# Decoder layer in float32: the maxima pass one unit behind the other stages, its row one unit earlier, value products one unit later

## What is computed

```python
def _L0_attn_ref(x, Wq, Wk, Wv, Wo):          # 16 heads, head width 32
    q, k, v = proj(Wq), proj(Wk), proj(Wv)
    scores = (einsum(q_r, k_r) + einsum(q_i, k_i)) / sqrt(16)
    scores = where(causal, scores, -inf)
    probs = softmax(scores, axis=-1)
    out = concatenate([probs @ v_r, probs @ v_i], axis=-1)
    return out.transpose(0, 2, 1, 3).reshape(B, N, 2 * C) @ Wo
...
x = x + _L0_attn_ref(_layernorm(x), Wq, Wk, Wv, Wo)
x = x + _L0_xattn_ref(_layernorm(x), ctx_1024, ctx_1024)   # a 16x16 causal softmax over heads, per token
x = x + _L0_ffn_ref(_layernorm(x), kernel, bias, a, b)     # quantized weight plus a low-rank term
```

## Time and profile before

| | |
|---|---|
| median of 3 runs | 923.08 us (922.64 to 927.23) |
| profiled execution | 918.79 us, span 917.0 us |
| TensorE (PE) busy | 708.1 us |
| VectorE (DVE) busy | 659.5 us |
| ScalarE (ACT) busy | 394.0 us |
| GpSimd (POOL) busy | 522.1 us |
| mean granted TensorE clock | 0.91 |

### The profile page before, as it was taken

How to read it: one execution, slowest core, us unless ns; L and a number is a source line. 1 busy time by engine, 2 the same in 40 slices (tenths; PEclk the granted TensorE clock), 3 DMA queues, 4 the chain that set the end, 5 groups by cost and what they waited for, 6 DMA issues and landing times.

```text
span 917.0 us, 14890 instructions
## 1 busy us (share of the span) xinstructions
PE 708.1 (77%) x5099; PEld 469.6 (51%) x5099; DVE 659.5 (72%) x1200; ACT 394.0 (43%) x750; POOL 522.1 (57%) x434
## 2 busy tenths in 40 slices
PE   2679898988898988998898889888989897351023
PEld 2455555745565555565666556655665564140022
DVE  3544354436667876889678977897769777989983
ACT  3114455344534545545544554455444553510101
POOL 4000000033667685668766786678676876867972
PEclk9779999999999989999999999999999998775555
DMA  4786566556575557555655665566565600101000
GB/s 150 101 106 93 70 91 84 104 65 78 78 117 76 75 76 122 75 72 104 100 88 76 103 94 93 78 103 99 66 80 105 99 2 25 40 6 34 0 22 24
DMA packets 47927, 70.46 MB, mean 77 GB/s; under 512 B 4849, under 2 KB 22530, under 8 KB 47874
## 3 DMA queue, kind: packets, MB, share of 16 engines
q1 hardware_dynamic: 46850, 69.52, 49.7%
q10 hardware_dynamic: 1024, 0.26, 0.3%
HBM read 14.98 MB, written 4.19 MB: 21 GB/s over the span
## 4 chain that ended last, share of the span: by engine, by line
PE 45%; DVE 18%; DMA 18%; issue 9%; ACT 7%; POOL 2%; ACTq 0%; DVEq 0%; SPq 0%; POOLq 0%
PE misc L427 22%; DMA stack_q<-max_row 16%; PE acc_bank L427 7%; PE exp_bank L427 6%; PE max_bank L427 6%; DVE head_out L839 4%; DVE neg_max L834 2%; ACT probs L668 2%; PE sum_bank L427 2%; DVE head_scores L839 2%; DVE prod L314 2%; DVE k_lo L896 2%; POOL prod L1093 2%; ACT misc L708 2%; DMA stack_k<-k_lo 1%
## 5 line engine op out<-in xcount | busy, mean ns | idle before, releaser
L668 ACT ACTIVATE probs<-exp_bank 128x512 f32<-128x512 f32 x320 | 188.0, 592 | 242.3 <-PE exp_bank L427 238.8
L1093 POOL TENSOR_TENSOR prod<-head_probs,ctx_sb 128x256 f32<-128x256 f32 (+3 forms) x128 | 236.0, 1876 | 23.9 <-DVE head_out L839 21.9
L834 DVE TENSOR_REDUCE neg_max<-max_bank 128x1 f32<-128x512 f32 (+1 forms) x192 | 130.7, 685 | 95.1 <-PE max_bank L427 94.4
L427 PE MATMUL exp_bank<-stack_q,stack_k 97*128 97x384 f32 (+3 forms) x512 | 151.1, 358 | 38.8 <-DMA stack_q<-max_row 35.5
L314 POOL TENSOR_TENSOR prod<-x1n,ctx_sb 128x256 f32<-128x256 f32 (+2 forms) x112 | 174.9, 1594 | 6.3 <-ACT x1n L638 5.4
L427 PE MATMUL acc_bank<-probs,values 128*32 128x512 f32 (+3 forms) x1024 | 159.3, 452 | 18.2 <-ACT probs L668 14.5
L427 PE MATMUL max_bank<-stack_k,stack_q 96*128 96x384 f32 (+3 forms) x512 | 156.8, 368 | 5.1 <-DVE neg_max L834 4.1
L427 PE MATMUL sum_bank<-probs,ones 128*32 128x512 f32 (+3 forms) x1024 | 159.6, 454 | 0.0
L834 DVE TENSOR_REDUCE seg_max<-max_bank 128x4 f32<-128x512 f32 x128 | 87.1, 687 | 86.4 <-PE max_bank L427 85.2
L1026 POOL TENSOR_TENSOR ln_var<-ln_mv,eps 128x4 f32<-128x4 f32 x24 | 5.2, 218 | 220.6 <-DVE ln_mv L820 220.6
L427 PEld LDWEIGHTS exp_bank<-stack_q,stack_k 97*128 97x128 f32 x512 | 84.6, 195 | 65.1 <-DMA stack_q<-max_row 33.9
(11 more groups left out here) (115 smaller groups left out, 1240.0 us busy)
## 6 DMA issues: line engine op xcount, KB each, us to landing
stack_q<-q_hi SPq DMA_DIRECT2D x64, 256.0 KB, 5.4
stack_k<-k_hi SPq DMA_DIRECT2D x64, 256.0 KB, 8.1
stack_q<-q_lo SPq DMA_DIRECT2D x32, 256.0 KB, 6.6
stack_k<-k_lo SPq DMA_DIRECT2D x32, 256.0 KB, 9.6
x_in<-in_x SPq DMA_DIRECT2D x8, 512.0 KB, 3.5
ctx_sb<-in_ctx SPq DMA_DIRECT2D x32, 128.0 KB, 2.8
x<-in_x SPq DMA_DIRECT2D x8, 512.0 KB, 7.4
out<-y_sb SPq DMA_DIRECT2D x8, 512.0 KB, 3.2
```

What stands on the lines that cost most here:

```text
L427: return nc.tensor.matmul(*args, **kw)
L668: nc.scalar.activation(probs[:, (UNITS * g + n) % PTR, :], exp_bank[n % 2][:, :], ACT.Exp, scale=SCALE).then_inc(exp_done, 1)
L834: vec.tensor_reduce(o, v, axis=AX_X, op=ALU.max, negate=True).then_inc(max_taken, 1)
L1093: last = gp.tensor_tensor(pv_prod[:, COFF[j]:COFF[j + 1]].rearrange("p (q d k) -> p q d k", q=4, k=keys), head_probs[:, 4 * j:4 * j + 4, N ...
```

## The change

The maxima pass runs one unit behind the loop (SHIFT 1), so that only its last unit falls into the next group. The transpose and ScalarE's copy and DMA of the row stand at unit 3, the latter two ahead of the inverses. `attend` runs one unit later (units n - 3 and n - 2 at n = 3, 5, 7, 9; units 8 and 9 at n = 1 of the next group), and so do the copies of `acc_bank` and the sums.

```diff
-    SHIFT = 3
+    SHIFT = 1
...
-                        if st["N"] and n == 0:
+                        if st["N"] and n == 1:
 
                             attend((8, 9), st["N"][1], first_tile - UNITS)
                         if st["C"]:
-                            if n == 2:
+                            if n == 3:
...
-                            if n in (2, 4, 6, 8):
-                                attend((n - 2, n - 1), st["C"][1], first_tile)
+                            if n in (3, 5, 7, 9):
+                                attend((n - 3, n - 2), st["C"][1], first_tile)
...
-                        if st["M"] and n == 4:
+                        if st["M"] and n == 3:
                             pe.wait_ge(max_ready, n_max_ready.up())
                             bank = take(0, max_row_ready, r_row)
...
-                        if st["N"] and n == 1:
+                        if st["N"] and n == 2:
 
                             act.wait_ge(pv_done, n_saved.up(UNITS))
...
+                        if st["M"] and n == 3:
+                            m_slot = st["M"][1]
+                            act.wait_ge(max_psum, n_row.up())
+                            wait(act, max_stacked, n_row_free.up(16) - 32)
+                            copy(max_row[:, m_slot % 2, :], misc[0][0:G * NT, 0:P]).then_inc(max_row_ready, 1)
...
                         if st["N"] and n == 4:
                             act.wait_ge(acc_saved, n_norm.now())
...
-                        if st["M"] and n == 5:
-                            m_slot = st["M"][1]
```

More of the change, by code:

```diff
@@ L693, in body @@
                             layernorm(2, x2, x2n, n - 2)
+                        if st["M"] and n == 3:
[3 more added lines that the diff above has]
+                            copy(max_row[:, m_slot % 2, :], misc[0][0:G * NT, 0:P]).then_inc(max_row_ready, 1)
+                            wait_apart(act, const_ready, (max_row_ready, n_row.now()))
+                            nc.scalar.dma_start(stack_q[STACK:STACK + 1, m_slot, :, :].bitcast(F32),
+                                                max_row[:, m_slot % 2, :].bitcast(F32)).then_inc(max_stacked, 16)
                         if st["N"] and n == 4:
```

## The result

The changed kernel takes 893.44 us (median of 4 runs, 892.81 to 894.8) against 922.86 (median of 4 of the kernel before): a ratio of 0.9684, 95% interval 0.9635 to 0.9732. The forecast was 890.4, range 862 to 912. The profiled execution took 894.05 us with a span of 892.2; the one before had 917.0, so the two traces differ by 24.8 us. The execution profiled before was a quick one: 31 later executions of that kernel took 921.2 to 928.1 us, with a mean granted TensorE clock of 0.906 to 0.896 where the profiled one has 0.910, so against its trace every gain looks some 5 us smaller than by the medians.

A forecast was written before the change was run, and what follows sets the result against it. It took TensorE, waiting for rows that land with their group's six loads, to bound the kernel before a VectorE and GpSimd tail. Seven terms sum to -32.7 us, 918.8 to 886.1; carried over to the median, 890.4 us, range 862 to 912.

The forecast's parts named there:

- Start-up: Before the first scores, the next group's first maxima unit moves ahead of both projections and waits for loads: +4.5 us.
- Wait for the row's copy: TensorE's 15 waits (20.4 us) for ScalarE's copy, which holds the value projection's PSUM bank, go: -18.0 us.
- The cover: Two pairs of units and an attend on TensorE, 2.4 us, hide ScalarE's copy and issue ahead of exponential 4.
- Half clock: TensorE's two 1.2 GHz stretches behind waits for the row's copy go, 1.5 us each: -3.0 us, bounds 0 and -3.4.
- Loads behind k_lo's: In three waiting groups the row overtakes a ctx load issued behind k_lo's, 1.4 us each: -4.2 us.
- nothing ahead of it changes: k_lo's load keeps its issue time, 2.09 us behind the k projection, so the row is issued 0.2 us behind it.
- rival A: The row gets ahead of k_lo's load in most groups, gaining up to 2.0 us each: 857 us, chance 0.20.
- groups with a late VectorE: Only groups where VectorE delays k_lo's load have the row issued ahead of it: 885 us, no separate chance given.
- Waits for `probs`: attend follows its exponential two units behind, not one, saving seven waits of 0.5 us in first groups: -3.7 us.
- costed at nothing: Moved attend calls (same count and banks, older probs), ScalarE's earlier copy and issue, and unit 1's load wait: 0 us.
- Fourth groups: Copy L887 meets shorter GpSimd operations (1.3 us) and the row is earlier (0.4), in four groups: -6.8 us.
- Near the end: TensorE's single 4.6 us wait for the maxima goes, but VectorE bounds right after: -1.5 us, bounds 0 and -4.6.

The follow-up runs named there:

- L887 alone: Kernel before the change, with the four-element copy at source line L887 made by a reduction over one element: 930.12 us, ratio 1.0062.
- the kernel with three edits: Changed kernel with attend calls back at their old units, start-up projections ahead of maxima units, and first groups' x copy and add later: 840.1 us.

## Why the prediction was right, and where it was not

The reading behind the forecast held: a waiting group waits for its six loads, and the row lands with whatever was issued just ahead of it. That the total came out within 3 us is in good part luck, since its parts missed by up to 25 us and cancelled. Point by point:

1. *Start-up*: +5.7 forecast at the first scores and +4.5 behind the next group; +3.6 measured at the first scores, +3.1 left at the fifth group. The cause (projections behind a maxima unit that waits 5.6 us) is shown. The row was forecast between the two k_hi loads; in four other traces it lands there, and the first scores start at 69.2 to 70.0, as forecast (69.3); in the changed kernel's it got ahead of both by luck.
2. *Wait for the row's copy*, -18.0: the wait went, the gain did not. The bank is free, and the step that failed is to book that as time: "nothing else holds that bank" looks at the bank alone. The cover named for ScalarE's copy and issue (2.4 us of TensorE's work) was not enough in first groups, where the copy of x and VectorE's add share the unit. In first groups, 14.9 us of waits went and the groups became 0.8 us longer.
3. *Half clock*, -3.0: between 72 and 700 us the stretches granted 0.50 went from 30.7 to 20.5 us, at most 5 us gained. Right in kind. What was not seen is that it can go the other way, as the runs with SHIFT 1 alone and with L887 alone showed.
4. *Loads behind k_lo's*: the row did pass the ctx loads, but the margin of 0.2 us holds only where VectorE is on time: "nothing ahead of it changes", said of k_lo's load, failed in second groups by 0.74 us. In steady second and fourth groups the row got ahead of k_lo's load, by 0.2 to 0.5 us, and landed 1.5 ahead of it; in third groups it stayed 0.26 us behind. That is rival A's case of "groups with a late VectorE", 885 us, so the forecast's mechanism and this rival's were both at work. Not every row lands as close behind as the 0.2 to 0.5 us that the text reads from two of them: of 29 in the trace of the kernel before, five landed 1.2 to 1.5 us behind the transfer issued just ahead of them, and one 0.17 us ahead of it.
5. *Waits for `probs`*, -3.7: the trace has five such places in first groups and not seven, of 0.75 us, which is the same sum. They went, but in first groups TensorE now waits 0.6 to 0.7 us for exponential 5's bank, at the same number of places; and moving `attend` behind the k projection cost 33 us of what the row could have gained. That the moved calls are "costed at nothing" is the largest error of the text.
6. *Fourth groups*: -6.8 forecast, -8.2 measured, for another reason. L887 did fall from 2.00 to 0.30 us in steady fourth groups. With L887 short and the row late these groups keep 19.5 us, with L887 at 2.01 and the row early they have 17.7: what counts there is the row's order against k_lo's load.
7. *Near the end*: -1.5 forecast; the last full third group went from 22.5 to 17.7 us, -4.8. VectorE did not bind right after. On the kernel with three edits the same place is worth 7 (SHIFT 3 against 1).

The forecast came out because first groups, which fell 25 us short of the sum, were met by second groups (10 us more than in it), third ones (3.5), fourth ones (1.4) and a start-up 2.1 us cheaper: 17 of the 25. The 8 left over shrank to 3, because the medians are 4.6 us further apart than the two profiled executions.

## What to carry to other kernels

When a small transfer is slow, look at what was issued ahead of it on all queues: its place in that order, in fractions of a microsecond, may be worth more than its issue time. Moving work on one engine is not free because that engine has slack: ask between which two issues it comes to stand, and cost each moved block against the transfers behind it. When a wait is removed, check each engine in the chain to the next exponential, copies of other stages included, before its length is booked as gain. And when a total comes out, compare its parts: here the missed ones led to three edits worth 53 us.

## What the runs showed of the hardware

- Loads issued on SyncE's queue and one row on ScalarE's queue land in the order of their issue, some 2 us apart for 256 KB (2.06 in most places). Over all 13 traces some 2300 pairs of a row and another transfer (loads, x and ctx) are issued from 0.1 us to a few us apart, and all but 14 of them land in the order of issue. In the changed kernel rows 0.18 to 0.20 us behind k_lo's load landed 0.17 to 0.37 behind it seven times and 0.11 and 0.20 ahead of it twice. Within 0.1 us the order of issue decides nothing: at 0.01 to 0.05 behind a load the row landed 1.4 to 2.1 us ahead of it in 114 of 117 places, at 0.06 to 0.09 behind it in 2 of 15, and once, 0.03 ahead, it landed behind. Nothing here tells what decides between. The Trainium skill (DMA: Bandwidth & Descriptors, section Queues, rings and completion order) has each DMA engine take turns between queue rows; these traces do not agree, with 6.1 to 10.8 us for 8 KB among loads in the two kernels against 1.8 unloaded.
- A four-element copy on VectorE took 2.00 us beside GpSimd's product (512.33 to 514.74) and ended with it; a reduction over one element gives the same numbers in 0.15 us beside the same product. The Trainium skill (SBUF — State Buffer, section SBUF: two separate sides) says that the port pair of the two is locked for a whole instruction, by VectorE's fast copies too; this agrees.
- The same kernel takes 921.2 us where the mean granted clock is 0.906 and 928.0 where it is 0.896. Freeing VectorE by 1.85 us at one place in some batches made it 6.5 us slower, at a mean of 0.896 against 0.903, with stretches of 3.4 us at half TensorE clock behind longer single waits; that these waits cause them is not shown.
